# Inverse square roots of the unit norms and layernorms as one power on GpSimd instead of Newton chains on VectorE

## The chip, the cores and the metric

The kernel runs on one core of one Trainium2 chip. A core has five engines that run side by side and wait for each other by semaphores: TensorE (matrix products, called PE in the profile, its weight loads PEld), VectorE (DVE), ScalarE (ACT), GpSimd (POOL) and SyncE (SP, which only issues DMAs here). The metric is the device time of one execution in microseconds, over several runs.

## The reference, cut to what matters

One transformer layer on 2048 tokens of width 512. The attention has 16 heads of 32, with unit norms on queries and keys; a mixture of 8 experts (two for each token) and a shared expert follow; after either part the input is added and a layernorm is taken.

```
def _unit_norm(t):
    return t * jax.lax.rsqrt(jnp.sum(t * t, axis=-1, keepdims=True) + 1e-06)
q, k = _unit_norm(q), _unit_norm(k)            # for each token and head
q, k = [m * _apply_rope(a, cos, sin) + (1.0 - m) * a for a in (q, k)]   # even heads alone are rotated
logits = jnp.einsum('bshd,bthd->bhst', q, k) * q_gain[None, :, None, None]
y = softmax(causal(logits)) @ v @ w_out

def _layernorm(x, axis=-1, eps=1e-05):
    m, v = jnp.mean(x, axis=axis, keepdims=True), jnp.var(x, axis=axis, keepdims=True)
    return (x - m) / jnp.sqrt(v + eps)
x = _layernorm(x + attention(x))
x = _layernorm(x + experts(x) + shared(x))
```

## The kernel before, in words

All tokens lie in 16 tiles of 128 rows; four tiles make a chunk of 512. Every product of float32 numbers is made as three products of split numbers (a high part, and a low part that is the remainder), so each operand is split by ScalarE (high) and VectorE or GpSimd (low).

**Attention, up to about 564 us.** Four groups of four heads; in each a loop of 40 slots (`SLOTS`), one slot for each pair of a chunk of queries and a tile of keys. TensorE makes the scores (L1351, masked by L1354), ScalarE the exponentials (L1479), TensorE the products with the values (L1376); sums of the exponentials are made by TensorE (L1373) or gathered on VectorE in `key_sum` (L1600). Tables written by hand put the other work into slots: `PROJECT_AT` (the products that give queries, keys and values, L1302), `NORMALISE_AT`, `ROTATE_AT`, `TURN_AT`. Chunks 0 and 1 of a group are prepared in the slots 25 to 39 of the group before, chunks 2 and 3 in its own slots 1 to 14. For each of the 16 pairs of group and chunk ScalarE copies queries and keys and squares them (L1435, L1439, L1443); VectorE sums the squares (L1551), adds the epsilon (L1553), takes the inverse square root of 128x32 numbers by `dve_rsqrt` and multiplies the half of the queries by the gain (L1558), all this in `dve_norms`; then `dve_rotate` multiplies queries and keys (L1567) and VectorE rotates the queries, GpSimd the keys (L1578 to L1584). ScalarE's next squares share an area with the rotation's products and wait for both. In the opening `OPENING` and `OPENING_LOW` give the order of TensorE's and VectorE's work.

`dve_rsqrt` (L1528) has no instruction for an inverse square root: a shift and a subtraction from a constant give a guess, and three Newton rounds of three instructions improve it. Each of the eleven waits for the one before it:

```
for _ in range(3):
    nc.vector.scalar_tensor_tensor(work, out, -0.5, out, ALU.mult, ALU.mult)
    nc.vector.tensor_tensor(work, work, arg, ALU.mult)
    nc.vector.scalar_tensor_tensor(out, work, 1.5, out, ALU.add, ALU.mult)
```

**Projection stage, 564 to about 626 us.** For each tile t TensorE multiplies with the output weights (L484) into one of two banks, VectorE adds the input (L854) into one of four buffers `rows` and takes statistics (L856). After tiles 3, 7, 11 and 15 `layernorm` (L808) makes the inverse deviations of a chunk (128x4 numbers) by `dve_rsqrt` and the scaled means (L821); `act_norm` (L764, L768) on ScalarE then normalises four tiles and so frees the buffers `rows` for the next chunk. ScalarE (L705) and GpSimd (L1112) split the tiles of the attention's output; GpSimd's queue holds only these subtractions here. TensorE begins tile t after VectorE has added tile t-2.

**Router, experts.** The first half of the shared expert runs while VectorE makes the router's choices; GpSimd scatters the rows by indirect DMAs (L1127); then 39 tiles go through the experts, up to about 1016 us. GpSimd splits the weights.

**Second half of the shared expert, to the end.** For each chunk c TensorE makes three blocks of hidden columns (L641) and then, after the first block of the next chunk, the four products down (L686) into two banks; VectorE multiplies (L919), takes remainders (L922), adds each product down to its tile and so frees the bank (L953), adds the two experts' rows of a tile (L979) as `EXTRAS_AT` and `EXTRAS_AFTER` say, takes statistics (L971), and calls `final_norm` for chunks 0, 1 and 2 in the blocks 5, 8 and 10 (`NORM_AT`), for chunk 3 at the end. GpSimd gathers the experts' rows in the order of tiles, two indirect DMAs for each (L1154), before tile t waiting for tile t-4 to be added and, at even t, for the gathers of the two tiles before to land.

Of the kernel before, what the change touches and what calls it, by code (L numbers as in the profile page):

```python
# [27 lines left out]
F32 = mybir.dt.float32  # L28
F32R = mybir.dt.float32r
BF16 = mybir.dt.bfloat16  # L30
I32 = mybir.dt.int32
# [5 lines left out]
P = 128  # L37
# [3 lines left out]
HG = 4  # L41
# [74 lines left out]
def build(nc, x, w_qkv, w_out, q_gain, gate_w, w_gate, w_up, w_down, sw_gate, sw_up, sw_down,  # L116
          rope_cos, rope_sin, numbers, out):
    with ExitStack() as ctx:
        def sem(name):
            return ctx.enter_context(nc.semaphore(name))  # L120
# [44 lines left out]
        shift = at("shift", 210176, [P, HEADS // 2], F32)  # L165
        sq_sum = at("sq_sum", 210208, [P, 2, TPC, HG], F32)
        inv_norm = at("inv_norm", 210464, [P, 2, TPC, HG], F32)
        newton = at("newton", 210592, [P, 2, TPC, HG], F32)
        shift_now = at("shift_now", 212128, [P, 2], F32)
        inv_col = at("inv_col", 210720, [P, CH // 32], F32)  # L170

# [14 lines left out]
        x_turned, xT_high, xT_low = sem("x_turned"), sem("xT_high"), sem("xT_low")  # L186
        w_loaded, w_high, w_low = sem("w_loaded"), sem("w_high"), sem("w_low")
        qkv_done, qkv_copied = sem("qkv_done"), sem("qkv_copied")
        norm_steps, inv_normed, sums_inverted = sem("norm_steps"), sem("inv_normed"), sem("sums_inverted")
        normed = sem("normed")  # L190
        q_products, k_products, q_roped, k_roped = sem("q_products"), sem("k_products"), sem("q_roped"), sem("k_roped")
        turned, turn_high, turn_low = sem("turned"), sem("turn_high"), sem("turn_low")
# [79 lines left out]
        var_eps = at("var_eps", 207488, [P, TPC], F32)  # L272
        rstd = at("rstd", 207520, [P, TPC], F32)
        mean_over = at("mean_over", 207584, [P, TPC], F32)
        ln_work = at("ln_work", 207552, [P, TPC], F32)
        place_int = at("place_int", 210784, [P, TOPK, NT], I32)
        tile_slot = at("tile_slot", 210912, [P, MAX_TILES], I32)
        tile_needs = at("tile_needs", 211072, [P, MAX_TILES], I32)
# [8 lines left out]
        ys_dram = nc.dram_tensor("y_sorted", [MAX_TILES * P, D], F32, kind="Internal").ap()  # L287
        half_dram = nc.dram_tensor("first_half", [T, D], F32, kind="Internal").ap()

        lot0_high, lot0_low, ln_ready = sem("lot0_high"), sem("lot0_low"), sem("ln_ready")  # L290
# [32 lines left out]
        def y_of(t):  # L323
            return y_raw[:, t % 4] if t >= TPC else y_first[t][:]
# [483 lines left out]
        def layernorm(n, c):  # L808

            for i in range(TPC):  # L810
                nc.vector.bn_aggr(moments[:, i], stats[:, i]).then_inc(ln_steps, 1)
            nc.vector.wait_ge(ln_steps, n + 4)
            nc.vector.tensor_scalar(var_eps[:], moments[:, :, 1], LN_EPS, None, ALU.add).then_inc(ln_steps, 1)
            nc.vector.wait_ge(ln_steps, n + 5)
            if c:

                nc.vector.wait_ge(x1_ready, min(TPC * c, NT))
            if c > NC:
                nc.vector.wait_ge(out_ready, TPC * (c - NC))
            dve_rsqrt(rstd[:], ln_work[:], var_eps[:], ln_steps, n + 5)  # L820
            nc.vector.scalar_tensor_tensor(mean_over[:], moments[:, :, 0], -1.0, rstd[:], ALU.mult, ALU.mult).then_inc(ln_ready, 1)  # L821

        LN_STEPS = 4 + 4 + 1 + 11
        CHOSEN_STEPS = 10
        TURN_LAG = 6
        PARTS_AT = [TURN_LAG + TPC, TURN_LAG + 2 * TPC]
# [12 lines left out]
        STATS_AT = [3, 6, 9]  # L839
        NORM_AT = [5, 8, 10]  # L840
        APPLY_AT = [5, 9, 11]
        LOT0_HIGH_AT = [8, 10, 12]
        LOT0_LOW_AT = [9, 10, 13]

# [262 lines left out]
        def tail_gpsimd(pool):  # L1107
            for t in range(NT):
                pool.wait_ge(y_high, t + 1)
                if t >= 2:  # L1110
                    pool.wait_ge(projected, t - 1)
                nc.gpsimd.tensor_tensor(y_l[:, t % 2], y_of(t), y_h[:, t % 2].bitcast(F32), ALU.subtract).then_inc(y_low, 1)  # L1112

            pool.wait_ge(x1_ready, NT)
            pool.wait_ge(router_steps, CHOSEN_STEPS)
            for piece in range(2):
# [30 lines left out]
            for t in range(NT):  # L1147
                if t >= 4:
                    pool.wait_ge(extras_added, TOPK * (t - 3))
                if t and t % 2 == 0:  # L1150
                    for landed in (t - 2, t - 1):
                        pool.wait_ge(gathered[landed % 4], 32 * (landed // 4 + 1))
                for k in range(TOPK):
                    nc.gpsimd.indirect_dma_start(out=extra[:, t % 4, k], out_offset=None, in_=ys_dram,  # L1154
                                                 in_offset=bass.IndirectOffsetOnAxis(ap=place_int[:, k, t:t + 1], axis=0)).then_inc(gathered[t % 4], 16)

        x_rows = x.rearrange("b s d -> (b s) d")
        block = ctx.enter_context(nc.Block())
# [293 lines left out]
        def act_copy_y(g, i):  # L1452
            step = NC * g + i
            nc.scalar.wait_ge(pv_done, SLOTS * g + STEP_AT[i + 1])
            if later(g) or i >= 2:
                nc.scalar.wait_ge(y_stored[i % 2], 16 * (NC // 2 * g + i // 2))
            elif i == 0:
                nc.scalar.wait_ge(norm_steps, 13 + 1)
            nc.scalar.copy(y_norm[:, i % 2, :], y_ps[:]).then_inc(y_copied, 1)

        def act_exp(g, slot):
# [66 lines left out]
        def dve_rsqrt(out, work, arg, ready, steps):  # L1528

            n = steps  # L1530
            for do in range(2):
                if do == 0:
                    nc.vector.tensor_scalar(out.bitcast(I32), arg.bitcast(I32), 1, None, ALU.arith_shift_right).then_inc(ready, 1)
                else:
                    nc.vector.tensor_scalar(out.bitcast(I32), out.bitcast(I32), -1.0, RSQRT_GUESS, ALU.mult, ALU.add).then_inc(ready, 1)
                n += 1
                nc.vector.wait_ge(ready, n)
            for _ in range(3):
                nc.vector.scalar_tensor_tensor(work, out, -0.5, out, ALU.mult, ALU.mult).then_inc(ready, 1)
                nc.vector.wait_ge(ready, n + 1)  # L1540
                nc.vector.tensor_tensor(work, work, arg, ALU.mult).then_inc(ready, 1)
                nc.vector.wait_ge(ready, n + 2)
                nc.vector.scalar_tensor_tensor(out, work, 1.5, out, ALU.add, ALU.mult).then_inc(ready, 1)
                nc.vector.wait_ge(ready, n + 3)
                n += 3

        def dve_norms(g, c):

            C = NC * g + c
            nc.vector.wait_ge(qkv_copied, 4 * (C + 1))  # L1550
            nc.vector.tensor_reduce(sq_sum[:], squares_of(g, c)[:], AX, ALU.add).then_inc(norm_steps, 1)  # L1551
            nc.vector.wait_ge(norm_steps, 13 * C + 1)
            nc.vector.tensor_scalar(sq_sum[:], sq_sum[:], UNIT_EPS, None, ALU.add).then_inc(norm_steps, 1)  # L1553
            nc.vector.wait_ge(norm_steps, 13 * C + 2)
            if later(g) or c:
                nc.vector.wait_ge(normed, C)
            dve_rsqrt(inv_norm[:], newton[:], sq_sum[:], norm_steps, 13 * C + 2)
            nc.vector.tensor_tensor(inv_norm[:, 0], inv_norm[:, 0],  # L1558
                                    gain[:, bass.ds(HG * g, HG)].unsqueeze(1).broadcast_to([P, TPC, HG]),
                                    ALU.mult).then_inc(inv_normed, 1)  # L1560

        def dve_rotate(g, c):

# [108 lines left out]
        def pool_split_w(g):  # L1672
            nc.gpsimd.wait_ge(w_high, g + 1)
            nc.gpsimd.tensor_tensor(wqkv_l[:], wqkv_raw[:], wqkv_h[:].bitcast(F32), ALU.subtract).then_inc(w_low, 1)

        def pool_rotate(g, c):
            rotate(nc.gpsimd, 1, NC * g + c, c, k_products, k_roped)

# [17 lines left out]
        @block.gpsimd  # L1696
        def _(pool):
            nc.gpsimd.memset(zeros[:], 0.0).then_inc(zero_made, 1)
            nc.gpsimd.memset(ones_b[:], 1.0)
            nc.gpsimd.memset(ident[:], 0.0)  # L1700
            nc.gpsimd.memset(mask_b[:], 0.0)
            nc.gpsimd.memset(ident_b[:], 0.0)
            nc.gpsimd.memset(ones[:], 1.0).then_inc(mask_filled, 1)
            pool.wait_ge(mask_filled, 1)
            for m in (ident_b, ident):
                nc.gpsimd.affine_select(out=m[:], in_=m[:], compare_op=ALU.not_equal, fill=1.0, base=0,
                                        pattern=[[-1, P]], channel_multiplier=1)
            nc.gpsimd.affine_select(out=tri_b[:], in_=ones_b[:], compare_op=ALU.is_gt, fill=0.0, base=0,
                                    pattern=[[1, P]], channel_multiplier=-1).then_inc(tables_made, 1)

            nc.gpsimd.affine_select(out=mask_b[:], in_=mask_b[:], compare_op=ALU.is_ge, fill=MASKED, base=0,
                                    pattern=[[1, P]], channel_multiplier=-1).then_inc(consts_ready, 1)
            pool_split_w(0)
            pool.wait_ge(tables_loaded, 48)
            for c in range(2):
                pool_rotate(0, c)
            def group(g):
                for slot in range(SLOTS):
                    for gg, c, _ in work_at(ROTATE_AT, slot, g):
# [31 lines left out]
```

## Time and profile before

| | us |
|---|---|
| median of 3 runs | 1128.35 |
| lowest, highest | 1126.13, 1132.17 |
| the profiled execution | 1127.57 |
| its span in the trace | 1125.8 |
| TensorE busy (instructions) | 1076.9 (6362) |
| VectorE busy | 620.7 (1126) |
| ScalarE busy | 543.6 (900) |
| GpSimd busy | 338.3 (278) |

The span is that of the records of one execution, and busy times are sums within it. TensorE's matmuls are pipelined and their ends are modelled, so that a busy TensorE need not be at its peak. An idle time is given with the instruction that ended it. The granted clock is the share of full speed that TensorE was given.

### The profile page before, as it was taken

How to read it: one execution, taken by the hardware profiler on the slowest of the kernel's cores; microseconds unless marked ns; L12 is line 12 of the kernel's file. 1: busy time of each engine (PE TensorE's matmuls, PEld its weight loads, DVE VectorE, ACT ScalarE, POOL GpSimd, SP SyncE). 2: the span in 40 equal slices, each digit the busy share in tenths (PEclk: the TensorE clock that was granted, in tenths of full speed). 3: DMA queues.
4: the chain of work that ended last, by engine and by line, in shares of the span. 5: the costliest groups of instructions: out<-in, count | busy, mean ns of one | idle time of the engine just before them, and what ended most of it. 6: DMA issues, size and time to landing. Idle time of an engine off the chain costs nothing.

```text
span 1125.8 us, 18393 instructions
## 1 busy us (share of the span) xinstructions
PE 1076.9 (96%) x6362; PEld 765.7 (68%) x6363; DVE 620.7 (55%) x1126; ACT 543.6 (48%) x900; POOL 338.3 (30%) x278
## 2 busy tenths in 40 slices
PE   6899999999999999999999998989999999999996
PEld 6654656645666456654377675779999999998874
DVE  3557684685937868477768554322222222223776
ACT  3467775687756876578836421113322322331213
POOL 1211111111111221112343045770566664624430
PEclk9999999999999999999999997989999999999998
DMA  6345505453343713337064016553444343423433
GB/s 188 112 130 160 142 31 142 135 163 104 86 123 92 204 59 94 113 103 216 1 210 146 1 38 218 204 190 110 151 151 151 126 152 102 138 82 106 138 105 112
DMA packets 106099, 141.61 MB, mean 126 GB/s; under 512 B 12784, under 2 KB 57328, under 8 KB 106032
## 3 DMA queue, kind: packets, MB, share of 16 engines
q1 hardware_dynamic: 89808, 103.48, 31.0%
q10 hardware_dynamic: 10944, 19.93, 5.1%
q0 software_dynamic: 5280, 17.31, 4.7%
q8 instruction: 42, 0.69, 0.3%
q14 instruction: 25, 0.20, 0.1%
HBM read 84.59 MB, written 56.10 MB: 125 GB/s over the span
## 4 chain that ended last, share of the span: by engine, by line
PE 81%; DVE 10%; ACT 6%; issue 2%; DMA 0%; SPq 0%; ACTq 0%; DVEq 0%
PE scores L568 14%; PE scores L1351 13%; PE bank L1302 12%; PE bank L1376 9%; PE bank L561 7%; PE scores L641 6%; PE bank L686 6%; ACT probs L1479 4%; PE bank L1373 4%; PE scores L484 2%; DVE x L979 2%; PE scores L583 2%; PE scores L1354 1%; DVE key_sum L1600 1%; PE bank L1331 1%
## 5 line engine op out<-in xcount | busy, mean ns | idle before, releaser
L1479 ACT ACTIVATE probs<-scores,shift_now 128x1024 f32<-128x1024 f32 (+3 forms) x296 | 272.9, 974 | 85.9 <-PE scores L1354 44.4
L1600 DVE TENSOR_TENSOR key_sum<-key_sum,probs 128x2048 f32<-128x2048 f32 (+3 forms) x92 | 192.7, 2094 | 58.4 <-ACT probs L1479 30.7
L1351 PE MATMUL scores<-q_stack,k_stack 96*128 96x512 f32 (+3 forms) x640 | 201.6, 416 | 5.6 <-ACT probs L1479 5.6
L1351 PEld LDWEIGHTS scores<-q_stack,k_stack 96*128 96x128 f32 x640 | 111.4, 192 | 138.2 <-ACT probs L1479 72.4
L568 PE MATMUL scores<-ffn_w,xt_h 128*128 x624 | 132.5, 335 | 4.6 <-issue 4.5
L1376 PE MATMUL bank<-probs,v_sb 128*32 128x512 f32 (+3 forms) x1184 | 135.7, 530 | 0.0
L1084 POOL TENSOR_TENSOR ffn_w<-raw,ones 128x1408 fp32r<-128x1408 f32 (+4 forms) x36 | 72.1, 2012 | 145.1 <-PE bank L561 103.2
L568 PEld LDWEIGHTS scores<-ffn_w,xt_h 128*128 128x128 f32 x624 | 103.8, 191 | 13.9 <-issue 11.8
L888 DVE TENSOR_TENSOR ht_l<-scores,ht_h 128x256 fp32r<-128x256 f32 x39 | 16.6, 425 | 146.7 <-ACT ht_h L753 146.7
L1088 POOL TENSOR_TENSOR ffn_w<-raw,ffn_w 128x1408 fp32r<-128x1408 f32 (+3 forms) x35 | 90.7, 2602 | 2.1
L641 PE MATMUL scores<-x1T_h,ffn_w 128*128 128x512 f32 x352 | 89.9, 392 | 0.0
L793 ACT CAST hid_h<-silu 128x512 fp32r<-128x512 f32 (+1 forms) x24 | 14.9, 620 | 125.1 <-DVE silu L919 125.0
L641 PEld LDWEIGHTS scores<-x1T_h,ffn_w 128*128 128x128 f32 x352 | 65.5, 188 | 14.4 <-issue 1.1
L686 PE MATMUL bank<-ffn_w,hid_h 128*128 128x512 f32 (+1 forms) x176 | 66.9, 435 | 7.8 <-DVE hid_l L922 5.1
L561 PE MATMUL bank<-ffn_w,ht_h 128*128 (+1 forms) x234 | 70.4, 409 | 0.0
L1302 PE MATMUL bank<-wqkv_h,xT_h 128*128 128x384 f32 x256 | 59.0, 353 | 5.1 <-ACT v_sb L1443 5.1
L568 PE MATMUL scores<-ffn_w,xt_l 128*128 x312 | 63.8, 327 | 0.0
L1578 POOL TENSOR_TENSOR rope_prod<-qk_even,cos 128x128 f32<-128x128 f32 x8 | 4.5, 556 | 197.3 <-DVE qk_even L1567 197.3
L1376 PEld LDWEIGHTS bank<-probs,v_sb 128*32 128x32 f32 x1184 | 29.7, 109 | 46.5 <-issue 39.9
L1589 DVE TENSOR_TENSOR turned_l<-bank,turned_h 128x512 fp32r<-128x512 f32 x32 | 22.1, 691 | 70.8 <-ACT turned_h L1450 70.7
L738 ACT CAST xt_h<-scores 128x512 fp32r<-128x512 f32 x39 | 22.8, 585 | 71.2 <-PE scores L583 71.2
L1354 PE MATMUL scores<-mask_b,ident_b 128*128 128x128 bf16 x256 | 57.2, 232 | 0.0
(223 smaller groups left out, 1793.6 us busy)
## 6 DMA issues: line engine op xcount, KB each, us to landing
q_stack<-turn_scratch SPq DMA_DIRECT2D x48, 256.0 KB, 3.8
k_stack<-turn_scratch SPq DMA_DIRECT2D x48, 256.0 KB, 4.1
x_sorted<-zeros SPq DMA_DIRECT2D x39, 256.0 KB, 3.0
y_sorted<-y_tile ACTq DMA_DIRECT2D x39, 256.0 KB, 2.3
x_tile<-x_sorted ACTq DMA_DIRECT2D x37, 256.0 KB, 2.7
turn_scratch<-turned_h SPq DMA_DIRECT2D x32, 256.0 KB, 2.1
turn_scratch<-turned_l SPq DMA_DIRECT2D x32, 256.0 KB, 2.5
raw<-w_gate SPq DMA_DIRECT2D x8, 704.0 KB, 5.4
```

Of the source, the lines that this page charges most:

```text
L561: mm = nc.tensor.matmul(out_tile[:], hs[0:kn, k, :], moving(slot_before, DOWN + (low * 3 + k) * D, D, kn), start=(m == 0 and k == 0), stop ...
L568: mm = nc.tensor.matmul(to[:, 0:FH], xs[:, k, :], moving(slot, first + (low * KC + k) * FH, FH), start=(m == 0 and k == 0), stop=(m == 2 a ...
L641: mm = nc.tensor.matmul(scores[:, which, n % 2, :], stationary(half, slot, which, low, k, hc), xs[:, k, c * CH:(c + 1) * CH], start=(m == ...
L686: mm = nc.tensor.matmul(bank[n % 2][:], hs[k0:k1, k, tt * P:(tt + 1) * P], shared_down(half, slot, low, k), start=(m == 0 and k == 0), sto ...
L1084: last = nc.gpsimd.tensor_tensor(high, src, one, ALU.mult)
L1088: last = nc.gpsimd.tensor_tensor(low, src, high.bitcast(F32), ALU.subtract)
L1302: mm = nc.tensor.matmul(qkv_ps[:, 0:3 * P], xs[:, k, tok], ws[:, k, :], start=(m == 0 and k == 0), stop=(m == 2 and k == KC - 1))
L1351: mm = nc.tensor.matmul(scores[:, p, hh, lo:CH], k_stack[0:3 * HD, h, j * P:(j + 1) * P], q_stack[0:3 * HD, i % 2, h, lo:CH], start=True, ...
L1354: mm = nc.tensor.matmul(scores[:, p, hh, lo:lo + P], ident_b[:], mask_b[:], start=False, stop=True)
L1376: mm = nc.tensor.matmul(y_ps[HD * h:HD * (h + 1), lo:CH], v_sb[:, j, HD * h:HD * (h + 1)], exponents(g, slot)[:, h, lo:CH], start=(j == 0) ...
L1479: nc.scalar.activation(exponents(g, slot)[:, 2 * p:2 * p + 2, lo:CH], scores[:, p, :, lo:CH], ACT.Exp, bias=shift_now[:, p:p + 1]).then_in ...
L1600: nc.vector.tensor_tensor(key_sum[:, :, lo:CH], key_sum[:, :, lo:CH], probs[:, slot % 4, :, lo:CH], ALU.add).then_inc(sum_dve, 1)
```

## The change

`dve_rsqrt` is gone. Its tile `newton` gives its place to `minus_half`, a column of -0.5, and `ln_work` is dropped. For a unit norm VectorE sums the squares and adds the epsilon; GpSimd raises 128x32 numbers to the power -0.5 in one instruction and multiplies the queries' half by the gain. In GpSimd's program this stands behind the rotations of the same slot. For a layernorm VectorE adds the epsilon, GpSimd raises 128x4 numbers to the power (`pool_deviations`), and VectorE waits for it before the scaled means. In the projection stage `pool_deviations` stands behind GpSimd's subtractions for tiles 5, 9, 13 and 15; at the end it stands behind the gathers of tile 11 for chunk 0, and behind those of tile 15 for chunks 1 to 3.

```
-        newton = at("newton", 210592, [P, 2, TPC, HG], F32)
+        minus_half = at("minus_half", 210592, [P, 1], F32)
...
             nc.vector.tensor_scalar(var_eps[:], moments[:, :, 1], LN_EPS, None, ALU.add).then_inc(ln_steps, 1)
-            nc.vector.wait_ge(ln_steps, n + 5)
...
-            dve_rsqrt(rstd[:], ln_work[:], var_eps[:], ln_steps, n + 5)
+            nc.vector.wait_ge(ln_powered, c + 1)
             nc.vector.scalar_tensor_tensor(mean_over[:], moments[:, :, 0], -1.0, rstd[:], ALU.mult, ALU.mult).then_inc(ln_ready, 1)
...
+        def pool_deviations(pool, c):
+            pool.wait_ge(ln_steps, LN_STEPS * (c + 1))
+            if c:
+                pool.wait_ge(x1_ready, min(TPC * c, NT))
+            if c > NC:
+                pool.wait_ge(out_ready, TPC * (c - NC))
+            nc.gpsimd.tensor_tensor(rstd[:], var_eps[:], minus_half[:].broadcast_to([P, TPC]), ALU.pow).then_inc(ln_powered, 1)
...
-        LN_STEPS = 4 + 4 + 1 + 11
+        LN_STEPS = 4 + 4 + 1
...
+        POWER_AT = [TPC + 1, 2 * TPC + 1, 3 * TPC + 1]
+        FINAL_POWER_AFTER = 11
...
                 nc.gpsimd.tensor_tensor(y_l[:, t % 2], y_of(t), y_h[:, t % 2].bitcast(F32), ALU.subtract).then_inc(y_low, 1)
-
+                if t in POWER_AT:
+                    pool_deviations(pool, POWER_AT.index(t))
+
+            pool_deviations(pool, NC - 1)
...
+                if t == FINAL_POWER_AFTER:
+                    pool_deviations(pool, NC)
+            for c in range(1, NC):
+                pool_deviations(pool, NC + c)
...
         def dve_norms(g, c):
             C = NC * g + c
             nc.vector.wait_ge(qkv_copied, 4 * (C + 1))
+            if C:
+                nc.vector.wait_ge(inv_powered, C)
             nc.vector.tensor_reduce(sq_sum[:], squares_of(g, c)[:], AX, ALU.add).then_inc(norm_steps, 1)
...
-            dve_rsqrt(inv_norm[:], newton[:], sq_sum[:], norm_steps, 13 * C + 2)
-            nc.vector.tensor_tensor(inv_norm[:, 0], inv_norm[:, 0],
...
+        def pool_norms(g, c):
+            C = NC * g + c
+            nc.gpsimd.wait_ge(norm_steps, 2 * (C + 1))
+            if C:
+                nc.gpsimd.wait_ge(normed, C)
+            nc.gpsimd.tensor_tensor(inv_norm[:], sq_sum[:], minus_half[:].unsqueeze(2).unsqueeze(3).broadcast_to([P, 2, TPC, HG]),
+                                    ALU.pow).then_inc(inv_powered, 1)
+            nc.gpsimd.wait_ge(inv_powered, C + 1)
+            nc.gpsimd.tensor_tensor(inv_norm[:, 0], inv_norm[:, 0],
+                                    gain[:, HG * g:HG * (g + 1)].unsqueeze(1).broadcast_to([P, TPC, HG]),
+                                    ALU.mult).then_inc(inv_normed, 1)
...
             for c in range(2):
+                pool_norms(0, c)
                 pool_rotate(0, c)
...
                     for gg, c, _ in work_at(ROTATE_AT, slot, g):
                         pool_rotate(gg, c)
+                    for gg, c, _ in work_at(NORMALISE_AT, slot, g):
+                        pool_norms(gg, c)
```

## Rows read from the trace of the kernel before

**Rows 1.** Page, busy time of each engine, its share of the span and instructions.

```profile
PE 1076.9 (96%) x6362; PEld 765.7 (68%) x6363; DVE 620.7 (55%) x1126; ACT 543.6 (48%) x900; POOL 338.3 (30%) x278
```

**Rows 2.** Table by stretches; PEclk is the granted clock, x counts instructions.

```profile
184.00:318.00 134.00, 132.82 (x908) 77.42 (x907) 92.22 (x134) 94.25 (x142) 17.89 (x25) 1.00 0.42 118
...
582.90:587.00 4.10, 4.10 (x13) 3.12 (x14) 1.83 (x3) 1.67 (x3) 1.28 (x1) 0.66 0.71 210
...
742.00:749.20 7.20, 6.84 (x27) 6.83 (x28) 0.03 (x1) 0.46 (x1) 7.04 (x4) 0.58 0.44 147
...
1090.90:1093.00 2.10, 2.03 (x9) 1.69 (x10) 0.62 (x2) 0.00 (x0) 0.00 (x0) 1.00 0.03 8
```

**Rows 3.** Groups by line and shape: count, busy us, mean ns, idle before.

```profile
L1539 DVE SCALAR_TENSOR_TENSOR newton<-inv_norm 128x32 f32<-128x32 f32 x48 | 9.2, 192 | 1.6
```

**Rows 4.** Timeline, VectorE, a unit norm: start and duration in us first.

```profile
145.39 0.18 DVE L1553 TENSOR_SCALAR sq_sum<-sq_sum 128x32 f32<-128x32 f32 x1
...
148.27 1.22 DVE L1567 TENSOR_TENSOR qk_even<-qk_even,inv_norm 128x1024 f32<-128x1024 f32 x1
```

**Rows 5.** Timelines around the first and second final layernorm, three engines.

```profile
1061.16 0.17 DVE L813 TENSOR_SCALAR var_eps<-moments 128x4 f32<-128x4 f32 x1
...
1063.55 0.16 DVE L821 SCALAR_TENSOR_TENSOR mean_over<-moments,rstd 128x4 f32<-128x4 f32 x1
...
1063.30 0.94 POOL L1154 DMA_INDIRECT extra<-y_sorted,place_int  x1 [3.21 <-DMA extra<-y_sorted,place_int]
...
1067.04 0.95 POOL L1154 DMA_INDIRECT extra<-y_sorted,place_int  x1 [0.30 <-issue]
...
1064.37 0.50 PE L686 MATMUL bank<-ffn_w,hid_h 128*128 128x512 f32 x1 [0.35 <-DVE x L953]
...
1090.97 0.50 PE L686 MATMUL bank<-ffn_w,hid_h 128*128 128x512 f32 x1 [1.82 <-DVE x L953]
```

**Rows 6.** Timelines around the first layernorm of the projection stage, four engines.

```profile
577.39 0.20 DVE L813 TENSOR_SCALAR var_eps<-moments 128x4 f32<-128x4 f32 x1
...
579.02 1.28 DVE L1543 SCALAR_TENSOR_TENSOR rstd<-ln_work,rstd 128x4 f32<-128x4 f32 x1
...
580.93 0.16 DVE L821 SCALAR_TENSOR_TENSOR mean_over<-moments,rstd 128x4 f32<-128x4 f32 x1
...
576.28 1.29 POOL L1112 TENSOR_TENSOR y_l<-y_raw,y_h 128x512 fp32r<-128x512 f32 x1 [1.43 <-ACT y_h L705]
...
579.00 1.29 POOL L1112 TENSOR_TENSOR y_l<-y_raw,y_h 128x512 fp32r<-128x512 f32 x1 [1.43 <-ACT y_h L705]
...
581.13 2.93 ACT L768 ACTIVATE x<-rows,mean_over,rstd 128x512 f32<-128x512 f32 x4 [2.21 <-DVE mean_over L821]
...
582.87 1.16 PE L484 MATMUL scores<-wo_h,y_h 128*128 128x512 f32 x4 [1.94 <-DVE rows L854]
```

**Rows 7.** Timeline, GpSimd, its product of 128x32.

```profile
543.20 0.24 POOL L1103 TENSOR_TENSOR gw_split<-gw_raw,ones 128x32 fp32r<-128x32 f32 x1
```

**Rows 8.** Timelines in the attention: GpSimd's rotation, ScalarE's copy, TensorE's projection.

```profile
152.18 2.50 POOL L1584 TENSOR_TENSOR qk_even<-rope_prod 128x128 f32<-128x128 f32 x1
...
155.05 0.26 ACT L1443 COPY v_sb<-bank 128x128 f32<-128x128 f32 x1
...
155.36 0.96 PE L1302 MATMUL bank<-wqkv_h,xT_h 128*128 128x384 f32 x4
```

**Rows 9.** Waits: who waited for whom, us in total, times, longest.

```profile
ACT squares L1439 <- POOL qk_even L1584: 6.1, 7, 1.0
```

**Rows 10.** Timelines behind the second and third layernorm of the projection stage.

```profile
598.81 1.17 PE L484 MATMUL scores<-wo_h,y_h 128*128 128x512 f32 x4 [1.29 <-DVE rows L854]
...
615.62 0.70 PE L484 MATMUL scores<-wo_h,y_h 128*128 128x512 f32 x2 [1.43 <-DVE rows L854]
...
597.07 2.23 ACT L768 ACTIVATE x<-rows,mean_over,rstd 128x512 f32<-128x512 f32 x3 [1.61 <-DVE mean_over L821]
```

**Rows 11.** Timeline, TensorE, idle time behind the third final layernorm.

```profile
1109.53 0.47 PE L686 MATMUL bank<-ffn_w,hid_h 128*128 128x512 f32 x1 [0.58 <-DVE hid_l L922]
```

More of the change, by code:

```diff
@@ L188, in build @@
         qkv_done, qkv_copied = sem("qkv_done"), sem("qkv_copied")
-        norm_steps, inv_normed, sums_inverted = sem("norm_steps"), sem("inv_normed"), sem("sums_inverted")
+        norm_steps, inv_powered, inv_normed, sums_inverted = sem("norm_steps"), sem("inv_powered"), sem("inv_normed"), sem("sums_inverted")
         normed = sem("normed")
@@ L274, in build @@
         mean_over = at("mean_over", 207584, [P, TPC], F32)
-        ln_work = at("ln_work", 207552, [P, TPC], F32)
         place_int = at("place_int", 210784, [P, TOPK, NT], I32)
@@ L288, in build @@
         half_dram = nc.dram_tensor("first_half", [T, D], F32, kind="Internal").ap()
-        lot0_high, lot0_low, ln_ready = sem("lot0_high"), sem("lot0_low"), sem("ln_ready")
+        lot0_high, lot0_low, ln_ready, ln_powered = sem("lot0_high"), sem("lot0_low"), sem("ln_ready"), sem("ln_powered")
         wo_loaded, wo_high, wo_low = sem("wo_loaded"), sem("wo_high"), sem("wo_low")
@@ L1457, in act_copy_y @@
             elif i == 0:
-                nc.scalar.wait_ge(norm_steps, 13 + 1)
+                nc.scalar.wait_ge(norm_steps, 2 + 1)
             nc.scalar.copy(y_norm[:, i % 2, :], y_ps[:]).then_inc(y_copied, 1)
@@ L1526, in dve_split_w @@
             nc.vector.tensor_copy(wqkv_h[:], wqkv_raw[:]).then_inc(w_high, 1)
[L1528 to L1545, printed above, removed]
         def dve_norms(g, c):
@@ L1550, in dve_norms @@
             nc.vector.wait_ge(qkv_copied, 4 * (C + 1))
+            if C:
+                nc.vector.wait_ge(inv_powered, C)
             nc.vector.tensor_reduce(sq_sum[:], squares_of(g, c)[:], AX, ALU.add).then_inc(norm_steps, 1)
-            nc.vector.wait_ge(norm_steps, 13 * C + 1)
+            nc.vector.wait_ge(norm_steps, 2 * C + 1)
             nc.vector.tensor_scalar(sq_sum[:], sq_sum[:], UNIT_EPS, None, ALU.add).then_inc(norm_steps, 1)
-            nc.vector.wait_ge(norm_steps, 13 * C + 2)
-            if later(g) or c:
-                nc.vector.wait_ge(normed, C)
-            dve_rsqrt(inv_norm[:], newton[:], sq_sum[:], norm_steps, 13 * C + 2)
-            nc.vector.tensor_tensor(inv_norm[:, 0], inv_norm[:, 0],
-                                    gain[:, bass.ds(HG * g, HG)].unsqueeze(1).broadcast_to([P, TPC, HG]),
-                                    ALU.mult).then_inc(inv_normed, 1)
         def dve_rotate(g, c):
@@ L1702, in _ @@
             nc.gpsimd.memset(ident_b[:], 0.0)
+            nc.gpsimd.memset(minus_half[:], -0.5)
             nc.gpsimd.memset(ones[:], 1.0).then_inc(mask_filled, 1)
```

## The prediction, made before the change was run

> **What bounds the kernel now.** I read the page's busy times first: TensorE is busy 96% of the span, VectorE 55%, GpSimd 30% [rows 1]. So taking work off VectorE pays only where TensorE stands still because of VectorE. The table by stretches says where that is. In a middle group of the attention TensorE is busy 132.82 of 134.00 us [rows 2], so there is almost nothing to win there, whatever VectorE is spared. Idle time lies in the projection stage (565 to 626 us) and in the second shared half at the end (1063 us on), and the layernorms are there. The waits and the timelines then show which instruction ends each idle time.
>
> **The removed work and its length.** One unit norm loses its eleven chained VectorE steps of 0.19 us [rows 3] and a product with the gain. Read on the timeline: the epsilon is added by 145.57 and the rotation's first product starts at 148.27 [rows 4], so the chain is 2.70 us long. There are 16 of them, some 43 us of VectorE. One layernorm loses eleven steps on 128x4. At the end of the kernel its chain runs from 1061.33 to the start of the last step, 1063.55, so 2.22 us [rows 5]. In the projection stage it runs from 577.59 to 580.93, so 3.34 us [rows 6]: one step of 0.16 us lasted 1.28 us just while GpSimd ran its subtraction of 1.29 us.
>
> **The price of a power.** No row shows one. GpSimd's product of 128x32 takes 0.24 us [rows 7] and its subtraction of 128x512 takes 1.29 us [rows 6], so one step costs (1.29 - 0.24) / 480 = 2.2 ns per element over a base of 0.2 us. The low end is a power as cheap as a product, 0.24 us on 128x32. A power of a variable number needs a logarithm, a product and an exponential, which I put at 25 steps (my guess): 0.2 + 32 x 25 x 2.2 ns = 2.0 us on 128x32 and 0.4 us on 128x4. The high end is 50 steps, 3.7 us and 0.6 us. I take 2.0 and 0.4. A hop between engines is 0.04 us where ScalarE starts at 581.13 after a VectorE step that ends at 581.09 [rows 6]; I take 0.1 us each way.
>
> A row and a rule part here. GpSimd's product of 128x32 takes 0.24 us where VectorE's step on the same shape takes 0.19 [rows 3, 7], a ratio of 1.3. The Trainium skill (GPSIMD Engine Reference, Engine selection) says not to put elementwise arithmetic there, as two-input operations are about twice as slow as on VectorE. By that rule the eleven steps' 2.4 us would be an estimate of 4.9 us on GpSimd, and the sum below would be some 20 us worse (7 places of the next part, 2.7 us each).
>
> **Unit norms in the attention.** The new chain is 0.1 + 2.0 + 0.24 (gain) + 0.1, and some 0.1 for the wait between the two GpSimd steps: 2.5 us against 2.70. Where the rotation follows at once, it starts 0.2 us earlier. That is worth nothing: TensorE's next projection starts at 155.36, as its scores end [rows 8]. But a longer chain would be paid in full: GpSimd's last rotation step ends at 154.68, ScalarE's squares waited for it (7 such waits, 6.1 us [rows 9]), its copy ends at 155.31 and the projection that needs the bank starts at 155.36. So there are 7 places with no slack. VectorE's freed 2.7 us elsewhere go into its waits. GpSimd has nothing queued behind the power but the rotation. Term: 0.
>
> **First layernorms (projection stage).** In the first of them GpSimd's queue is free at 577.6, as its subtraction for tile 5 is over when the epsilon is added; the power starts there and the last step starts at about 577.7 + 0.4 + 0.1 = 578.2 instead of 580.93. ScalarE would then be late next: it idled 2.21 us before its normalisation at 581.13, so it can start at 578.92, and VectorE's sum of tile 4, which waits for the first of its four tiles, comes 2.2 us earlier. TensorE idled 1.94 us for that sum [rows 6]. This idle time goes, and with it what followed: the granted clock was 0.66 of full (partly the 1.2 GHz level) over the 4.10 us after it [rows 2], so 4.10 x 0.34 = 1.4 us. The second and third layernorms have idle times of 1.29 and 1.43 us before the projections at 598.81 and 615.62, and ScalarE idled 1.61 us before its normalisation at 597.07 [rows 10], which is the room. The fourth has no idle time behind it. Sum: -(1.94 + 1.29 + 1.43) - 1.4 = -6.1 us. At worst the power starts late behind tile 5's or 9's subtraction and half comes, -3.
>
> **Last layernorms (second shared half).** Here the change moves the power past a queue. In GpSimd's program it stands behind the gathers of tile 11. The first final layernorm has its epsilon added at 1061.33, and VectorE goes on at 1063.55. GpSimd's gathers of tiles 10 and 11 start at 1063.30, as they wait for earlier gathers to land and not for VectorE, and the last is issued from 1067.04 to 1067.99 [rows 5]. So the power can't start before 1068.0, and the last step starts at 1068.0 + 0.1 + 0.4 + 0.1 = 1068.6 or, with the 0.3 us that follow an indirect issue, 1068.8: VectorE is 5.2 us late. Queued behind it are the sums that free the banks, for which TensorE already waited 0.35 us at 1064.37. TensorE takes the 5.2 us in full, since VectorE is its limit up to 1090.97, where it waited 1.82 us [rows 5]. After an idle time of some 5.6 us the clock will be low for a while: 1.4 us lost as above, at most what the stretch 742.00:749.20 shows, 7.20 x 0.42 = 3.0 us [rows 2], at least 0. For the other three final layernorms GpSimd's gathers are out by then, also when shifted (the last pair needs tile 11 added, some 3.5 us before the second epsilon). Each chain shrinks from 2.22 to 0.7 us: -1.5 for the second, which is on the path; for the third only the 0.58 us that TensorE idled behind it [rows 11], -0.6; -1.5 for the fourth, which ends the kernel. Sum: 5.2 + 1.4 - 1.5 - 0.6 - 1.5 = +3.0 us, from +1.6 to +4.6 with the clock.
>
> The other edits cost nothing: one more fill on GpSimd of a 128x1 tile while it waits for weights, fewer semaphore steps, and no DMA more or less.
>
> **Sum.** 0 - 6.1 + 3.0 = -3.1 us. On the profiled execution (1127.57 us, span 1125.8) that is 1124.5; it stands 0.8 us under the median of the runs, 1128.35, so I forecast 1125.3. A measurement of this kernel can tell about 0.5% from no change, 5.6 us: the forecast is "within".
>
> **Rivals.**
> *A dear power.* Place: the seven spots of the attention with no slack, and then the opening. Price: 7 us for each us by which the power on 128x32 passes 2.2 us. It eats the whole gain from 2.6 us on and makes the kernel slower by over 0.5% from 3.4 us. At 4.0 us it gives -3.1 + 7 x 1.8 = +9.5, so 1137.9. For it: a software function on an engine with a base of 2.2 ns per element and step, of unknown step count. Against: 128 partitions are worked side by side, as 1.29 us for 128x512 show. The skill's rule named above is on this side.
> *The gain in the projection stage doesn't come.* ScalarE's or the loads' order takes the place of the removed wait. Then only the tail is left, +3.0, so 1131.4. Against: ScalarE's idle times before its normalisations.
> *The tail stall is mild and the power cheap.* If the power is near 0.24 us and the clock stays up after the gap, the sum is -6.1 + 1.6 and 1.5 us (a guess) in the opening and the attention: -6.0, 1122.4. For it: after the idle 1.82 us at 1090.97 the clock stayed full [rows 2, 5]. Against: it fell after the idle 1.94 us at 582.87 [rows 2, 6].
>
> **How the numbers follow.** Forecast 0.57, with its own range 1122 to 1129; dear power 0.22; no gain in the projection stage 0.10 (nearly all within 0.5%); mild tail 0.11. Faster by over 0.5% (under 1122.7): the last case and a little of the forecast, 0.17. Slower by over 0.5% (over 1134.0): most of the dear power, 0.22. Within: 0.61. The low end is that of the mild tail, 1121.5; the high end takes in a power of about 4 us, 1138, and leaves out one in ten above it.
>
> **What would show it.** Right: powers on GpSimd of 2.0 and 0.4 us; TensorE's idle times before the projections of tiles 6, 10 and 14 gone, the clock full there; a new idle time of 5 to 6 us in TensorE after the second down block of the last half, with VectorE waiting for a power that starts as the gather of tile 11 ends; three shorter final chains; attention groups of the same length. Wrong: squares on ScalarE that wait over 1 us longer for GpSimd's rotation, or longer groups (dear power); or the first final layernorm let through before the gathers.

## The result: 1177.49 us, 4.4% slower, and the profile after

| | before | changed |
|---|---|---|
| median of 4 runs, us | 1127.71 | 1177.49 |
| lowest, highest | 1126.13, 1132.17 | 1175.21, 1178.42 |
| ratio, 95% interval | | 1.0437, 1.0406 to 1.0467 |
| span of the profiled execution | 1125.8 | 1175.6 |

The forecast was 1125.3 with a range from 1121.5 to 1138.0. First the busy times of the changed kernel (the answer to [rows 1]):

```profile
PE 1093.0 (93%) x6362; PEld 775.9 (66%) x6363; DVE 568.0 (48%) x846; ACT 543.4 (46%) x900; POOL 445.4 (38%) x319
```

VectorE gave up 52.7 us of work, GpSimd took on 107.1, and TensorE, with as many instructions, is busy 16.1 us longer: its clock was lower for a while. Next GpSimd's groups by line and shape, and the waits with their total, number and longest:

```profile
L1674 POOL TENSOR_TENSOR inv_norm<-sq_sum,minus_half 128x32 f32<-128x32 f32 x16 | 86.8, 5426 | 290.5 <-DVE sq_sum L1552 290.5
L828 POOL TENSOR_TENSOR rstd<-var_eps,minus_half 128x4 f32<-128x4 f32 x8 | 8.1, 1017 | 35.0 <-DVE var_eps L812 34.8
```

```profile
DVE qk_even L1559 <- POOL inv_norm L1677: 45.2, 8, 5.8
ACT squares L1455 <- POOL qk_even L1576: 35.4, 7, 6.2
PE bank L1318 <- ACT v_sb L1459: 30.4, 14, 4.6
```

A power takes 5.43 us on 128x32 and 1.02 us on 128x4. Read from the top, the three waits are one chain: VectorE waits for the power, the squares wait for the keys' rotation on GpSimd (35.4 us where it was 6.1 [rows 9]), TensorE waits for the bank that ScalarE then frees.

The table by stretches, as in [rows 2], cut at the same points of the program in both kernels. Before: the opening, the four groups of the attention, the projection stage, the first shared half with the router, the experts, the end.

```profile
0.00:50.35 50.35, 38.02 (x205) 34.16 (x206) 25.17 (x63) 18.11 (x51) 11.42 (x27) 1.00 0.54 157
50.35:177.90 127.55, 123.92 (x850) 69.53 (x851) 90.60 (x130) 92.18 (x133) 16.18 (x23) 1.00 0.43 123
177.90:311.59 133.69, 132.51 (x911) 77.11 (x904) 91.96 (x133) 93.99 (x141) 17.90 (x26) 1.00 0.42 119
311.59:445.26 133.67, 132.49 (x910) 77.12 (x904) 91.95 (x133) 93.99 (x141) 17.89 (x26) 1.00 0.42 119
445.26:564.28 119.02, 117.14 (x824) 59.16 (x817) 78.25 (x90) 86.42 (x116) 26.97 (x26) 1.00 0.36 103
564.28:626.21 61.93, 56.45 (x268) 44.26 (x265) 48.36 (x109) 29.22 (x47) 19.33 (x15) 0.97 0.51 162
626.21:742.36 116.15, 107.73 (x434) 77.13 (x432) 52.73 (x159) 25.70 (x40) 52.84 (x43) 0.94 0.37 136
742.36:1019.89 277.53, 275.76 (x1585) 251.83 (x1586) 70.70 (x155) 80.42 (x195) 142.87 (x64) 0.99 0.40 129
1019.89:1125.80 105.91, 92.87 (x405) 75.33 (x403) 70.95 (x158) 23.62 (x37) 32.94 (x32) 0.97 0.39 120
```

And the changed kernel:

```profile
0.00:51.62 51.62, 38.04 (x205) 33.94 (x206) 20.67 (x39) 18.14 (x52) 22.80 (x32) 1.00 0.51 153
51.62:190.10 138.48, 128.13 (x850) 72.27 (x851) 79.10 (x76) 92.16 (x133) 38.95 (x27) 0.96 0.39 113
190.10:338.04 147.94, 137.49 (x911) 79.75 (x904) 83.02 (x84) 93.99 (x142) 42.45 (x34) 0.97 0.38 107
338.04:485.16 147.12, 136.89 (x911) 79.72 (x904) 83.01 (x84) 93.89 (x142) 42.43 (x34) 0.97 0.38 108
485.16:614.02 128.86, 120.41 (x824) 61.39 (x817) 77.10 (x71) 86.43 (x116) 42.04 (x34) 0.97 0.33 95
614.02:669.21 55.19, 54.37 (x268) 43.09 (x265) 39.94 (x75) 29.13 (x47) 22.41 (x18) 1.00 0.58 182
669.21:788.13 118.92, 107.98 (x434) 77.27 (x432) 50.65 (x148) 25.62 (x40) 53.26 (x44) 0.93 0.38 137
788.13:1064.53 276.40, 274.67 (x1585) 251.31 (x1585) 70.70 (x155) 80.40 (x195) 143.01 (x64) 0.99 0.39 127
1064.53:1175.60 111.07, 95.00 (x405) 77.16 (x403) 63.80 (x114) 23.61 (x37) 38.03 (x36) 0.95 0.37 114
```

The whole loss lies ahead of the projection stage: 614.02 against 564.28, +49.7 us. The projection stage is 6.7 us shorter, the end 5.2 longer. In the attention the first number less TensorE's busy time is what it stood still. For the group at 190.10 that is 10.45 us against 1.18, so 9.3 of the 14.25 us by which it is longer are idle time and 5.0 are the same matmuls at a lower granted clock. Over the whole 49.7 us it is 32.9 and 16.9.

Where TensorE stands still shows on its own timeline; these are all its idle times over 1 us from 160 to 240 us, a little over half a group's length:

```profile
166.01 0.96 PE L1318 MATMUL bank<-wqkv_h,xT_h 128*128 128x384 f32 x4 [2.97 <-ACT v_sb L1459]
...
193.91 0.66 PE L1347 MATMUL bank<-ident,qk_odd 128*128 128x128 f32 x4 [1.84 <-DVE qk_odd L1576]
...
233.15 1.65 PE L1318 MATMUL bank<-wqkv_h,xT_h 128*128 128x384 f32 x4 [4.57 <-ACT v_sb L1459]
```

They follow the norms of slots 28, 38 and 4. Slot 4 costs the most, for two reasons besides the power. The timeline around it on VectorE, GpSimd and ScalarE:

```profile
229.61 2.54 DVE L1592 TENSOR_TENSOR key_sum<-key_sum,probs 128x2048 f32<-128x2048 f32 x1
...
229.97 2.50 POOL L1576 TENSOR_TENSOR qk_even<-rope_prod 128x128 f32<-128x128 f32 x1
...
232.56 0.38 ACT L1455 ACTIVATE squares<-bank 128x256 f32<-128x256 f32 x1 [6.15 <-POOL qk_even L1576]
```

The last step of the keys' rotation on GpSimd lasts 2.50 us, beside a key sum of VectorE over 128x2048. Before, at the same place, it ended ahead of the key sum and took 0.45:

```profile
210.81 0.45 POOL L1584 TENSOR_TENSOR qk_even<-rope_prod 128x128 f32<-128x128 f32 x1
...
211.03 2.37 DVE L1600 TENSOR_TENSOR key_sum<-key_sum,probs 128x2048 f32<-128x2048 f32 x1 [0.51 <-issue]
...
211.35 0.38 ACT L1439 ACTIVATE squares<-bank 128x256 f32<-128x256 f32 x1 [1.03 <-POOL qk_even L1584]
```

The rotation is later by the power, the key sum isn't (its exponentials were there), so now they meet. Steps of 2.50 us are four in the kernel before, three of them at slot 28, and eight in the changed one: the four of slot 4 are new. The second reason is the clock, in a row of the table by stretches for the changed kernel:

```profile
232.70:238.00 5.30, 4.85 (x16) 4.56 (x16) 0.00 (x0) 3.02 (x7) 0.00 (x0) 0.50 0.00 0
```

After 4.57 us of idle TensorE the granted clock is 0.50, the 1.2 GHz level, up to 238.00, 4.85 us of busy TensorE (the stretch begins 0.45 us before the idle time ends).

### The profile page after: what moved, and what is told of

The parts are those of the page before. It is cut to its first block, busy times and chain, and to the rows that moved or that the text cites. A ratio compares the mean times of both kernels' runs of the same rounds, so it can differ in the third digit from the quotient of the medians.

```text
span 1175.6 us, 18176 instructions
## 1 busy us (share of the span) xinstructions
PE 1093.0 (93%) x6362; PEld 775.9 (66%) x6363; DVE 568.0 (48%) x846; ACT 543.4 (46%) x900; POOL 445.4 (38%) x319
## 4 chain that ended last, share of the span: by engine, by line
PE 67%; POOL 11%; DVE 9%; ACT 6%; issue 4%; DMA 2%; ACTq 0%; POOLq 0%; SPq 0%; DVEq 0%
PE scores L567 13%; PE bank L1318 10%; PE scores L1367 8%; PE bank L560 7%; PE bank L1392 6%; POOL inv_norm L1674 5%; PE scores L640 5%; PE scores L483 4%; PE bank L685 3%; ACT probs L1495 3%; PE bank L1389 2%; DVE key_sum L1592 2%; POOL x_sorted L1139 2%; POOL qk_even L1576 1%; PE scores L582 1%
## 5 line engine op out<-in xcount | busy, mean ns | idle before, releaser
L1674 POOL TENSOR_TENSOR inv_norm<-sq_sum,minus_half 128x32 f32<-128x32 f32 x16 | 86.8, 5426 | 290.5 <-DVE sq_sum L1552 290.5
L1318 PE MATMUL bank<-wqkv_h,xT_h 128*128 128x384 f32 x256 | 62.0, 366 | 30.4 <-ACT v_sb L1459 30.4
L1318 PEld LDWEIGHTS bank<-wqkv_h,xT_h 128*128 128x128 f32 x256 | 46.4, 200 | 36.9 <-ACT v_sb L1459 34.4
L1318 PE MATMUL bank<-wqkv_l,xT_h 128*128 128x384 f32 x256 | 58.9, 353 | 0.2 <-POOL wqkv_l L1666 0.2
```

What stands on the lines that cost most here:

```text
L1318: mm = nc.tensor.matmul(qkv_ps[:, 0:3 * P], xs[:, k, tok], ws[:, k, :], start=(m == 0 and k == 0), stop=(m == 2 and k == KC - 1))
L1674: nc.gpsimd.tensor_tensor(inv_norm[:], sq_sum[:], minus_half[:].unsqueeze(2).unsqueeze(3).broadcast_to([P, 2, TPC, HG]), ALU.pow).then_inc ...
```

## The experiments

Theory A: the length of the power is paid wherever a rotation follows it at once. B: the move to GpSimd's queue costs, whatever the operation. C: the meeting of rotation step and key sum is a cost of its own. Ratios are to the kernel before on the same chip; some chips ran both slower, so the ratios are compared.

**The two halves of the change.** The first run keeps `dve_rsqrt` in the unit norms, the second in the layernorms.

```
# first: dve_norms as before, no pool_norms    # second: layernorm as before, no pool_deviations
dve_rsqrt(inv_norm[:], newton[:], ...)         dve_rsqrt(rstd[:], ln_work[:], var_eps[:], ...)
```

> The kernel before with the powers in the eight layernorms alone; the unit norms keep their Newton chains on VectorE. Theory A (the loss is the unit norms' power, paid in the attention part; the layernorms give and take about the same): attention as before, projection stage -6.7 us, first shared half +2.8, tiles -1.1, tail +5.2 as in the changed kernel's trace: 1127.9 us. Rival (the tail and first shared half are longer in the changed kernel only because of what the attention part leaves behind): the +2.8 goes and the time is about 1125 us.

> The changed kernel with the layernorms back on their Newton chains; the powers stay in the sixteen unit norms. Theory A: the attention part keeps its whole +49.7 us and the rest is as before: 1177.4 us. Rival (part of the loss lies in the layernorms' powers): 1170 us or below.

Layernorms alone: 1125.54 us, ratio 0.9984 (0.9959 to 1.0009). Unit norms alone: 1178.32 us, ratio 1.0436 (1.0389 to 1.0484). The loss is the unit norms'. The spans ahead of the projection stage are 564.5 and 613.6 us. Of the first run 1127.9 was expected, with +2.8 us in the first shared half and router as in the changed kernel; in its trace they are 1.3 us shorter than before. By its time it can't be told from either expectation. That stretch, with the projection stage, took between 170 and 185 us in kernels with the same code there, by its clock and its waits, so the changed kernel's +2.8 in it can't be put down to the change. The projection stage by itself is firm: 55.0 to 55.5 us in all kernels with the powers there, 60.4 and 61.9 in the two without.

**A product in the power's place.** It leaves out the inverse root; engine, place in the queue and waits stay.

```
-nc.gpsimd.tensor_tensor(inv_norm[:], sq_sum[:], minus_half ..., ALU.pow)
+nc.gpsimd.tensor_tensor(inv_norm[:], sq_sum[:], small ..., ALU.mult)      # 0.0055
```

> The changed kernel, but each unit norm's power is a product with the constant 0.0055 on the same engine, at the same place in its queue, with the same waits; the inverse root of the unit norms is left out. Theory A (the length of the power): 5.42 us become about 0.3, the chain is shorter than the Newton chain, the attention part is as before or up to 8 us shorter: 1120 to 1128 us. Rival B (the move to GpSimd's queue and the extra crossings between engines cost, whatever the operation): at least half of the 49.7 us stays, 1153 us or more.

1126.74 us, ratio 0.9993 (0.9966 to 1.0020). Its groups by line and shape:

```profile
L1675 POOL TENSOR_TENSOR inv_norm<-sq_sum,small 128x32 f32<-128x32 f32 x16 | 3.8, 239 | 311.6 <-DVE sq_sum L1553 311.6
```

B falls: same engine, queue and waits, and the whole loss is gone. It shows too that the chain's shortening by some 2 us, to 0.24 + 0.22 us of work, wins nothing in the attention (564.9 us to its end, 564.3 before). A power as short as a product would not have paid in the unit norms either.

**VectorE waits for the keys.**

```
 dve_rotate(gg, c)
+nc.vector.wait_ge(k_roped, 2 * (NC * gg + c + 1))
```

> The changed kernel with one wait more: behind each rotation in the four groups VectorE waits until GpSimd has rotated the keys, so that its key sum can't run beside GpSimd's last rotation step. Theory C (that step takes 2.50 us instead of 0.45 beside the key sum, and ScalarE's squares wait for it): about 2 us less at each of the three slot-4 places, 6 us or a little more with the clock: 1171 us. Rival (the step's length is hidden or the later key sum takes its place): 1177 us, no change.

1167.75 us, ratio 1.0339 (1.0295 to 1.0383). One wait more on VectorE makes the kernel faster by 11 us, give or take 6, by the two ratios. The same place in its timeline, GpSimd, VectorE, TensorE:

```profile
226.93 0.45 POOL L1576 TENSOR_TENSOR qk_even<-rope_prod 128x128 f32<-128x128 f32 x1
...
227.41 2.29 DVE L1592 TENSOR_TENSOR key_sum<-key_sum,probs 128x2048 f32<-128x2048 f32 x1 [0.76 <-POOL qk_even L1576]
...
228.06 1.35 PE L1318 MATMUL bank<-wqkv_h,xT_h 128*128 128x384 f32 x4 [2.54 <-ACT v_sb L1459]
```

The step is back at 0.45 us and the idle time is 2.54 instead of 4.57 us, 2.03 less, as C has it. The wait keeps the two apart at slot 28 too, where they met in the kernel before: no last rotation step of GpSimd takes over 0.75 us any more, and the idle time behind slot 28, 2.97 us in the changed kernel, is 0.90:

```profile
163.11 0.97 PE L1318 MATMUL bank<-wqkv_h,xT_h 128*128 128x384 f32 x4 [0.90 <-ACT v_sb L1459]
```

The attention as one stretch:

```profile
0.00:607.88 607.88, 564.98 (x3681) 327.83 (x3682) 340.10 (x354) 384.86 (x581) 171.04 (x158) 0.97 0.39 111
```

It gained 6.1 us: 10.2 us of idle time less, and 4.0 us of busy TensorE more. Why the clock was no better with less idle time is open (0.97 and 0.95 in the last two groups). A further 3.5 us of the two profiled executions lie in the projection stage and the router, the stretch that varies by more than that, so the time of the run says little of C.

**Half a power, without and with that wait.**

```
+nc.gpsimd.tensor_tensor(inv_norm[:, 0], sq_sum[:, 0], minus_half ..., ALU.pow)
+nc.gpsimd.tensor_tensor(inv_norm[:, 1], sq_sum[:, 1], small ..., ALU.mult)
```

> The changed kernel with the power on the queries' half of the unit norms alone (128x16); the keys' half is a product with 0.0055, so the inverse root of the keys' norms is left out. The two take about 2.9 and 0.2 us. By the product run the attention part is flat up to a Newton chain's length (2.2 us of power). If the loss is in proportion beyond that, (3.1 - 2.2) / (5.42 - 2.2) x 49.7 = 14 us: 1141 us. If the first places have slack, and the clock's fall and the collision of the key sum with the rotation come only with a long power, 1 to 7 us: 1128 to 1134 us.

> The half-power kernel (128x16 of power, the keys' half a product, their inverse root left out) with the wait of the second run: behind each rotation VectorE waits for GpSimd's rotation of the keys. Theory C (beyond a Newton chain's length there are some 0.7 us of slack at slot 4; what made the half power cost 16 us is the last rotation step at 2.50 instead of 0.45 us, as the key sum now runs beside it): the 2.27 us of TensorE idle behind slot 4 goes to about 0.2, the clock stays at 1.00, 1126 to 1131 us. Rival (the length alone, in proportion): 1140 us or more.

The first: 1143.47 us, ratio 1.0124 (1.0083 to 1.0166); the second: 1139.77, ratio 1.0053 (1.0021 to 1.0085). The group of the half power, and the slot 4 place of the first kernel:

```profile
L1675 POOL TENSOR_TENSOR inv_norm<-sq_sum,minus_half 128x16 f32<-128x16 f32 x16 | 46.5, 2906 | 288.6 <-DVE sq_sum L1553 288.6
```

```profile
215.60 2.50 POOL L1577 TENSOR_TENSOR qk_even<-rope_prod 128x128 f32<-128x128 f32 x1
...
218.79 1.65 PE L1319 MATMUL bank<-wqkv_h,xT_h 128*128 128x384 f32 x4 [2.27 <-ACT v_sb L1460]
```

From the epsilon to the rotation it is now 3.50 us against the 2.70 of the prediction, 0.8 more. Slots 28 and 38 show no idle time over 0.7 us (0.60 the first time). Slot 4 shows 2.27 us. The clock behind it:

```profile
218.80:222.00 3.20, 3.20 (x10) 3.20 (x11) 0.00 (x0) 1.96 (x2) 0.00 (x0) 0.50 0.00 0
```

The first run's ratio comes to 14 us, just what the expectation gave for a loss in proportion to the power's length; the second run shows that this was luck. With the wait, the step is 0.45 again, slot 4 has no idle time over 0.7 us, and the attention ends at 568.0 instead of 582.9 us (564.3 before). So the collision made 15 of that kernel's 18.6 us in the attention, partly by the clock: it is 0.97 to 0.99 in the groups without the wait and 1.00 with it. The time shows less of it: by the two ratios 8 us, give or take 6, and 1.0053 is 1133.7 us at the pace of the first chip, between C's 1126 to 1131 and the rival's 1140. The projection stage and the router took 183.9 us in this trace and 173.6 in the other.

**One slot at a time.** `c not in (2,)`, `(3,)` and `(0, 1)` choose the chunks whose unit norm keeps the power; the others get the product.

> The changed kernel with the power of chunk 2 (the norm of slot 4 of each group) as a product with 0.0055; that inverse root is left out, the other twelve powers stay. From the changed kernel's trace: 4.57 us of TensorE idle behind slot 4 in groups 1 to 3 and some 2.5 us more by the clock's fall: 7.1 x 3 = 21 us less, 1156 us. Rival (the loss comes by the sum of GpSimd's time, a quarter of the powers bears a quarter of it): 12 us less, 1165 us.

> The changed kernel with the power of chunk 3 (slot 11) as a product; that inverse root is left out, the other twelve powers stay. In the changed kernel's trace its rotation comes at slot 14 and no engine on TensorE's path waits for it: 0 us less, 1177 us. Rival (as above, in proportion): 12 us less, 1165 us.

> The changed kernel with the powers of chunks 0 and 1 (the opening and slots 28 and 38) as products; those inverse roots are left out, the other eight powers stay. From the trace: three times 2.8 + 1.8 us of TensorE idle and 2.1 in the opening: 16 us less, 1161 us; with the clock and the exponentials that follow, up to the rest of the 49.7 us, 28 us less, 1149 us. Rival (in proportion, half): 25 us less. If the three kernels' gains sum to the 49.7 us, the places add; if they sum to more, one place's delay gives slack to the next.

Ratios 1.0177 (1.0092 to 1.0262), 1.0359 (1.0281 to 1.0436) and 1.0196 (1.0119 to 1.0273), on a chip that ran the kernel before at 1140.93 us. To the changed kernel's 1.0437 that is about 29, 9 and 27 us less, with some 10 us of uncertainty each. The traces say more. The attention of the first and the third run:

```profile
0.00:590.63 590.63, 555.24 (x3680) 321.83 (x3682) 342.53 (x354) 384.36 (x581) 159.97 (x159) 0.98 0.40 114
```

```profile
0.00:589.23 589.23, 551.36 (x3681) 323.31 (x3682) 342.97 (x354) 384.33 (x581) 146.19 (x159) 0.98 0.40 115
```

It ends 23.4 and 24.8 us earlier than in the changed kernel. In proportion to the powers it would be 12 and 25 us: slot 4 costs twice its share, and the other run can't tell the two apart. (The expectations count three places at slot 4; the first group's, with 3.77 us of idle time in the changed kernel, is a fourth.) Without slot 4's power its idle time is gone and the other two stand as they were; without those of slots 28 and 38 and the opening the reverse:

```profile
160.25 0.97 PE L1319 MATMUL bank<-wqkv_h,xT_h 128*128 128x384 f32 x4 [2.94 <-ACT v_sb L1460]
...
186.60 0.66 PE L1348 MATMUL bank<-ident,qk_odd 128*128 128x128 f32 x4 [1.83 <-DVE qk_odd L1577]
```

```profile
222.46 1.65 PE L1319 MATMUL bank<-wqkv_h,xT_h 128*128 128x384 f32 x4 [4.60 <-ACT v_sb L1460]
```

So the places are paid each for itself. Slot 11 was repeated on another chip (the profiled execution of the first comparison was the longest of its four):

> The same kernel as the one without slot 11's power, on another chip, as that comparison left 9 us +- 9 open. Theory A: as the changed kernel, ratio 1.044, 1177 us. Rival (in proportion): 1165 us.

Ratio 1.0394 (1.0355 to 1.0432). Its attention ends at 612.5 us against 614.0, with the idle times of the changed kernel. In proportion it would be 12 us less, which neither the trace nor the times allow: by the two ratios it is 5 us less, with some 5 us of uncertainty. In the traces the three gains are 23.4 + 24.8 + 1.6 = 49.8 us, the whole loss of 49.7, so the places add; in the times they are 61 us, with some 15 of uncertainty.

**The layernorms' queue.** The first run leaves the four final layernorms on Newton chains, the second has their powers and `FINAL_POWER_AFTER = 9` instead of 11; the unit norms are as before in both.

> The powers in the four layernorms of the projection stage alone; unit norms and the four final layernorms keep their Newton chains. Theory A (the projection stage gives some 7 us, the tail takes 5.2 because GpSimd has the gathers of tiles 10 and 11 ahead of the first final power): tail as before, 105.9 us, sum 1125.5 - 5.3 = 1120.3 us. Rival (the longer tail is something else, for instance all four final powers): not below 1124 us.

> Powers in all eight layernorms, Newton chains in the unit norms, and the first final power two tiles earlier in GpSimd's queue, behind the gathers of tile 9 instead of tile 11. Theory A: the first final layernorm waits about 1.2 us for its power instead of 7.85, TensorE's 6.0 us idle there goes, the other three keep their shorter chains: tail 104 to 105 us, sum about 1119 us. Rival (the gathers of tiles 10 and 11, issued later, are late for the additions behind the first layernorm): tail 107 us or more, 1121 us or above.

1121.12 us, ratio 0.9942 (0.9919 to 0.9965), and 1119.37 us, ratio 0.9919 (0.9888 to 0.9950): both are faster than both kernels. The first final layernorm, in the changed kernel and then with the power ahead of the gathers of tiles 10 and 11:

```profile
1111.68 0.95 POOL L1166 DMA_INDIRECT extra<-y_sorted,place_int  x1 [0.30 <-issue]
...
1112.65 1.05 POOL L828 TENSOR_TENSOR rstd<-var_eps,minus_half 128x4 f32<-128x4 f32 x1
...
1113.81 0.16 DVE L819 SCALAR_TENSOR_TENSOR mean_over<-moments,rstd 128x4 f32<-128x4 f32 x1 [7.85 <-POOL rstd L828]
...
1114.66 0.80 PE L685 MATMUL bank<-ffn_w,hid_h 128*128 128x512 f32 x1 [6.00 <-DVE x L962]
```

```profile
1057.62 1.04 POOL L829 TENSOR_TENSOR rstd<-var_eps,shift_and_half 128x4 f32<-128x4 f32 x1 [1.33 <-DVE var_eps L813]
...
1058.77 0.16 DVE L820 SCALAR_TENSOR_TENSOR mean_over<-moments,rstd 128x4 f32<-128x4 f32 x1 [1.24 <-POOL rstd L829]
...
1059.54 1.01 POOL L1167 DMA_INDIRECT extra<-y_sorted,place_int  x1 [0.87 <-DMA extra<-y_sorted,place_int]
```

The wait of 7.85 us is 1.24, TensorE's 6.00 us are gone, and the end takes 102.5 us instead of 111.1 (105.9 before), where 104 to 105 was expected. The kernel with all eight layernorm powers, above, differs from this one in the place of that power alone: 0.9984 against 0.9919, 7 us with some 5 of uncertainty. The end varies a little by itself: in the two runs that have the code of before there, it took some 2 us longer than before. No run has the power on VectorE.

## Why the prediction was wrong, step by step

- **The price of a power: the step that failed.** It took 2.0 us with a high end of 3.7; measured 5.42. The three shapes give 1.017, 2.906 and 5.426 us on 4, 16 and 32 numbers for each partition: a base of 0.39 us and 157 ns for each number. The base stood at 0.2. The 157 ns stood at 25 steps of 2.2 ns by a guess, 55 ns, and 50 steps at the high end, 110: no run shows that count, so the high end was no bound either. It set the term of the unit norms at 0, where the attention lost 49.7 us. The rival of a dear power named the right mechanism at 0.22, and the sign it gave came true: the squares wait 35.4 us for the keys' rotation where it was 6.1 [rows 9].
- **The cost of a us of power** was 7 us, from 7 waits without slack. At 5.42 us that rule gives 7 x 3.2 = 22.5 us; the attention lost 49.7. So the price alone wouldn't have mended it. At the seven places (slot 4 four times, slot 28 three times) TensorE's idle times are 3.77 + 3 x 4.57 and 2.97 + 2 x 2.65 us, 25.8 in all: near the rule, but by two errors that partly cancel, since the places have 0.2 to 1.4 us of slack each and slot 4 has 2 us of collision on top. The rest was in no number of the rival: 5.4 us behind slot 38, which reach TensorE through the queries' rotation and show in no wait of the squares, 2.1 in the opening, which it named without a price, and 16.9 by the clock. The prediction gave the clock's fall behind an idle time a price in the projection stage and the tail, and left it out of this rival.
- **"A cheaper chain wins nothing in the attention": right**, by the product's run.
- **Projection stage: right.** -6.1 predicted, -6.7 in the trace; the idle times before the projections of tiles 6, 10 and 14 are gone and the clock is 1.00. The powers took 1.02 us instead of 0.4; VectorE's wait of 1.1 to 1.2 us per layernorm was still shorter than ScalarE's room.
- **The end: right in kind, its size within the spread.** +3.0 predicted, +5.2 in the trace; against the two other kernels with the end of before it is +3.0 and +3.3. The stall stood where it was put, behind the gather of tile 11, and cost TensorE 6.00 us. The later chains shrank from 2.22 to some 1.25 us, not 0.7, by the dearer power.
- **Layernorms together**: forecast 1125.3, and the kernel with them alone measured 1125.54. That it is so near is in part luck: its interval is 3 us to either side, and in the trace -6.7 and +5.2 stand where -6.1 and +3.0 were predicted. What was wrong is the one term set at 0. The low end of the range, 1121.5, was said to be that of the mild tail, whose own sum is 1122.4; nothing hangs on it.
- **The Trainium skill's rule** (GPSIMD Engine Reference, Engine selection) spoke against the change and was right in sign. Its ratio of 2, put on the eleven steps, gave an estimate of 4.9 us, near the measured 5.42, by luck: the 5.42 us are one power and not eleven steps at twice their length, and on one product of 128x32 the ratio is 1.3 [rows 3, 7]. Its sum of some 20 us was short for the reasons above.

## What to carry to other kernels

Ask what one instruction costs before it takes the place of a chain: eleven instructions of 0.19 us beat one of 5.42. Where no row prices an operation, a guessed step count bounds nothing, so the range must reach until it hurts, with the clock's fall and the engines that will now meet counted in. And a step moved to another queue should be placed ahead of that queue's long waits: the same power two tiles earlier turned +5.2 us at the end into -3.4 in the traces.

## What the runs showed of the hardware

- GpSimd's power of float32 took 1.017, 2.906 and 5.426 us on 4, 16 and 32 numbers of a partition, one line of 0.39 us + 157 ns for each number; its product of 128x32 takes 0.24 us in all. The exponent was -0.5 throughout.
- A GpSimd step with two inputs on 128x128 lasted 2.50 us instead of 0.45 wherever it started inside VectorE's sum of two inputs over 128x2048, four times before and eight times after, each time 0.36 us into a sum of some 2.54; beside a sum over 128x512 of 0.94 us it lasted 0.90. Steps that met only the sum's first 0.2 us kept their length (0.45 and 0.59 us), and beside VectorE's rotation steps, two inputs of 128x128, GpSimd's took 0.49 to 0.59. The kernel before has the meeting at slot 28, with slack behind it [rows 8]. The Trainium skill (GPSIMD Engine Reference, Specifications) says that GpSimd shares its SBUF interfaces with VectorE and that they contend when VectorE reads two inputs from SBUF. The trace agrees for the long sums. By 2.50 - 0.45 it would have been worth some 2 us per slot 4 place in the prediction.
- The granted clock was 0.50 over the 4.85 us of busy TensorE behind 4.57 us of idle time. With half a power it was 0.50 in the 3.2 us behind 2.27 us of idle time. In the four groups of the kernel before, and in those of half a power with the wait, it was 1.00; their longest idle time is 1.49 us.
